# A stack of four graph layers on one core: the third layer's new rows are transposed by SyncE's transfers, and the two products behind them change places

## The reference

```python
h = relu(layernorm(x)); x = x + attention(h, adj)               # 4 heads
h = relu(layernorm(x)); x = x + (h @ W_self + (adj @ h / deg) @ W_neigh)
h = relu(layernorm(x)); x = x + gru(relu((adj @ h) @ W_msg.T + b_msg), h)
h = relu(layernorm(x)); x = x + hyperbolic(h, adj)
```

## Time and profile before

| | |
|---|---|
| median of three runs | 601.5 us (601.31 to 602.59) |
| the profiled execution | 602.1 us |
| its span | 600.3 us |
| TensorE busy | 560.5 us, 93% of the span |
| VectorE busy | 338.8 us, 56% |
| ScalarE busy | 211.4 us, 35% |
| GpSimd busy | 100.1 us, 17% |
| third layer with this pattern | about 310 to 450 us |

### The profile page before, as it was taken

One profiled execution on the slowest core, in us unless ns is written; L12 is line 12 of the kernel. 1 busy time (PEld: TensorE's weight loads), 2 busy tenths in 40 slices (PEclk: granted clock), 3 DMA queues, 4 the chain that ended last, 5 costly groups with the idle time before them and its releaser, 6 DMA issues.

```text
span 600.3 us, 12084 instructions
## 1 busy us (share of the span) xinstructions
PE 560.5 (93%) x4535; PEld 351.5 (59%) x4535; DVE 338.8 (56%) x1483; ACT 211.4 (35%) x580; POOL 100.1 (17%) x104
## 2 busy tenths in 40 slices
PE   4679899999999999999999999999999999999981
PEld 3578799999994544444444545554554444555540
DVE  4882372333323563333314687788779763676876
ACT  4530011100011110000032478778778555532433
POOL 3870100000000010000001112212122210330322
PEclk9979999999999999999999999999999999999996
DMA  8999999999940000000000001100100020110000
GB/s 230 108 108 108 106 109 108 108 108 108 109 44 4 5 14 0 1 0 1 19 0 19 18 26 30 36 13 25 36 1 20 17 86 3 36 55 36 18 36 35
DMA packets 23897, 29.17 MB, mean 49 GB/s; under 512 B 11296, under 2 KB 11936, under 8 KB 23840
## 3 DMA queue, kind: packets, MB, share of 16 engines
q0 software_dynamic: 8704, 16.78, 27.8%
q1 hardware_dynamic: 15136, 11.62, 6.4%
HBM read 72.43 MB, written 4.19 MB: 128 GB/s over the span
## 4 chain that ended last, share of the span: by engine, by line
PE 82%; DVE 10%; issue 3%; POOL 1%; ACT 1%; DMA 1%; SPq 0%; DVEq 0%; POOLq 0%
PE acc L1565 50%; PE acc L1375 9%; PE acc L1376 9%; PE acc L1405 4%; PE acc L1412 3%; PE acc L1395 1%; PE acc L1463 1%; PE acc L1462 1%; PE acc L1461 1%; DMA x<-x_rows 1%; POOL rs L1029 1%; PE acc L1497 1%; DVE hs_a L372 1%; PE acc L1468 1%; DVE mean L414 1%
## 5 line engine op out<-in xcount | busy, mean ns | idle before, releaser
L1565 PE MATMUL acc<-adj,hs_a 128*128 128x512 fp8e4 x1024 | 227.7, 379 | 2.8 <-DVE hs_a L561 2.0
L1565 PEld LDWEIGHTS acc<-adj,hs_a 128*128 128x128 f16 x1024 | 99.3, 98 | 116.7 <-DVE hs_a L561 2.2
L1375 PE MATMUL acc<-region_op,adj 128*128 128x133 f16 x1024 | 127.1, 224 | 5.0 <-issue 3.6
L1376 PE MATMUL acc<-region_op,adj 128*128 128x132 f16 x1024 | 127.2, 223 | 0.0
L1565 PE MATMUL acc<-adj,region_op 128*128 128x512 fp8e4 x512 | 118.3, 379 | 0.0
L1375 PEld LDWEIGHTS acc<-region_op,adj 128*128 128x128 fp8e4 x1024 | 100.9, 99 | 6.5 <-issue 3.7
L1376 PEld LDWEIGHTS acc<-region_op,adj 128*128 128x128 fp8e4 x1024 | 100.8, 98 | 0.1
L1565 PEld LDWEIGHTS acc<-adj,region_op 128*128 128x128 f16 x512 | 49.3, 98 | 56.7 <-issue 4.0
L1029 POOL TENSOR_TENSOR region_st<-region_st,small 128x4 f32<-128x4 f32 (+1 forms) x39 | 44.9, 1151 | 204.3 <-ACT w L1167 131.3
L1029 POOL TENSOR_TENSOR rs<-rs,small 128x4 f32 (+3 forms) x27 | 30.9, 1147 | 267.9 <-DVE rs L389 251.4
L1146 ACT ACTIVATE hs_a<-rowbuf 128x512 f32 (+1 forms) x8 | 5.0, 630 | 117.3 <-DVE rowbuf L395 117.3
(11 more groups left out here) (239 smaller groups left out, 682.7 us busy)
## 6 DMA issues: line engine op xcount, KB each, us to landing
adj<-adj_pieces POOLq DMA_DIRECT2D x32, 512.0 KB, 66.2
p_rows<-rowbuf SPq DMA_DIRECT2D x8, 256.0 KB, 2.0
region_op<-p_rows SPq DMA_DIRECT2D x8, 256.0 KB, 3.1
out_rows<-x SPq DMA_DIRECT2D x7, 256.0 KB, 2.0
x<-x_rows SPq DMA_DIRECT2D x3, 512.0 KB, 7.6
region_st<-matrices SPq DMA_DIRECT2D x1, 768.0 KB, 9.8
x<-x_rows SPq DMA_DIRECT2D x2, 256.0 KB, 4.4
hT<-region_op SPq DMA_TRANSPOSE x32, 2.3
```

Of the source, the lines that this page charges most:

```text
L1375: mm(bank[TG + it % TG][:, 0:HI], adj8[:, it, jt, :], op0[:, jt, 0:HI], start=(jt == 0), stop=False)
L1376: last = mm(bank[TG + it % TG][:, 0:LO], adj8[:, it, jt, :], op0[:, jt, HI:OPW], start=False, stop=(jt == NT - 1))
L1565: last = mm(dst, hs[:, jt, part, :], adj8[:, c * TG:(c + 1) * TG, jt, :], start=(k == 0), stop=(k == 2 * NT - 1))
```

## The change

For the groups 0 to 6 the eight transposes of the new rows are no longer matmuls and a copy but eight transposing transfers of SyncE from `row16` to `h3T16`, counted by a new semaphore `new_in`. They wait for `row16_ready` and for the embedding before (`emb_full`); in SyncE's stream they stand behind the store of the group before and ahead of the own rows of three groups later. Group 7 keeps TensorE's transposes and ScalarE's copy. Embedding and own product change places: `embed` at k = 50, `own_part` at k = 54, so behind `update_back` at 53. In the written out list both come behind 12 matmuls of the second aggregation of the last layer, and `update_back` of group 7 behind six of them. ScalarE's high half of a group's new rows waits until the transfers of the group before have landed.

```diff
+            def transpose_new_rows(g):
+                sp.wait_ge(S["row16_ready"], g + 1)
+                if g:
+                    sp.wait_ge(S["emb_full"], g)
+                for part in range(2):
+                    for t in range(TG):
+                        sp.dma_start(h3T16[:, part, t * D:(t + 1) * D], row16[:, part, t, :],
+                                     transpose=True).then_inc(S["new_in"], 16)
+
             sp.sem_inc(S["p1_out"], 16)
-            for g in range(NG):
-                transpose_own_rows(g)
-                if g > 2:
-                    store_p1(g - 3)
-            for g in range(NG - 3, NG):
-                store_p1(g)
+            transpose_own_rows(0)
+            transpose_own_rows(1)
+            for p in range(1, NG + 3):
+                if p >= 3:
+                    store_p1(p - 3)
+                if 0 <= p - 2 < NG - 1:
+                    transpose_new_rows(p - 2)
+                if p + 1 < NG:
+                    transpose_own_rows(p + 1)
...
             def high_rows(g):
                 act.wait_ge(S["xnew_ready"], g + 2 * NG + 1)
+                if g:
+                    act.wait_ge(S["new_in"], g * OWN_IN)
...
             def rows_T(g):
-                act.wait_ge(S["h3_tr"], g + 1)
+                act.wait_ge(S["h3_tr"], 1)
...
-                if second:
+                if i - 2 == NG - 1:
                     rows_T(i - 2)
...
+            def new_columns(s):
+                if s == 2 * NG - 1:
+                    pe.wait_ge(S["h3T_ready"], 1)
+                else:
+                    pe.wait_ge(S["new_in"], (s - NG + 1) * OWN_IN)
+
             def embed(s):
-                pe.wait_ge(S["h3T_ready"], s - NG + 1)
+                new_columns(s)
...
             def own_part(s):
-                pe.wait_ge(S["h3T_ready"], s - NG + 1)
+                new_columns(s)
...
-            late = {15: new_transposes, 43: own_part, 48: embed}
+            late = {50: embed, 54: own_part}
...
             aggregate(FIRST, 0, 36)
+            aggregate(SECOND, 0, 6)
+            update_back(FIRST - 1)
+            aggregate(SECOND, 6, 12)
+            embed(FIRST - 2)
             own_part(FIRST - 2)
-            embed(FIRST - 2)
-            update_back(FIRST - 1)
-            aggregate(SECOND, 0, 40)
+            aggregate(SECOND, 12, 40)
```

More of the change, by code:

```diff
@@ L233, in build_graph_stack @@
             "top_ready", "topall_ready", "w16_ready", "odd_ready", "odd_sum", "flag_ready", "turn", "gen_in",
-            "pre_tr", "pre_hT", "hidden_full", "sum_ready", "agg_full", "aThi_ready", "aT_ready", "l1_self", "self_read", "l1_neigh",
+            "pre_tr", "pre_hT", "hidden_full", "new_in", "sum_ready", "agg_full", "aThi_ready", "aT_ready", "l1_self", "self_read", "l1_neigh",
             "msg_full", "msg_ready", "gates_full", "rz_ready", "t_ready", "n_ready", "u_ready", "uT_full",
```

## The result

The changed kernel is **slower**: 604.3 us (median of 20 runs) beside 601.4 us for the kernel before (20 runs), ratio 1.0051 with a 95% interval of 1.0035 to 1.0068, so about 3.1 us. I had forecast 0.7 us less, 600.8, in a range up to 603.0. It went the way of rival C. The profiled executions have spans of 603.2 and 600.3 us.

What follows compares the result with a forecast made beforehand. TensorE was taken to bound the kernel, busy 93% of the span. Six periods each save 0.44 us less a 0.31 us wait, minus 0.05 for the order: 0.7 us less, 601.5 to 600.8, range 598.8 to 603.0.

Steps and rivals of the forecast that it cites:

- rival C: SyncE's queue, 97% occupied: closely packed sets take 10.68 us, each period 0.53 us longer; +3.2 us, 604.7; chance 0.17.
- The chain to the low half: VectorE's low half of the new rows, which releases the new transfers: no earlier step moves, ready at T0 + 4.94.
- T0: The first matmul of an aggregation on TensorE, from which the prediction counts the times in a period.
- An undisturbed set: SyncE's eight new transfers: start at T0 + 5.03, 10.02 us to issue, last landing T0 + 16.2; TensorE waits 0.31 us.
- Group 6's share: Handover to the next layer: TensorE waits for VectorE anyway, wait grows from 1.17 to 1.7 us, seventh 0.44 us lost.
- Its late embedding: Group 6's embedding, 3.8 us later: last rows start at T0 + 22.9 instead of 21.14, hidden before TensorE needs them.
- rival D: Handover slips: group 6's later embedding delays group 7's tangent, TensorE waits; price 0.3 to 1 us, about 601.5; chance 0.08.
- The queue's room: SyncE's queue: two sets and the store, 20.4 us plus 0.2 us waking, fit a period of 21.07 us.
- far bound: Upper limit for the new set's length on SyncE: the slowest set of the trace, 10.68 us, 0.66 us more.
- signs of being wrong: Low half at another distance from T0, a set other than 10.0 us, or VectorE taking TensorE's place in a period.
- The Trainium skill against the exchange: Page's 390 ns per transpose on TensorE against 1309 ns by DMA: speaks against the change; set estimated 0.4 us longer.

Runs made afterwards that it cites:

- the table of doses: Zero, 4, 6, 7 or 8 of a group's new-row transposes as transfers, against the kernel before: ratios 1.0003, 0.9971, 0.9966, 0.9972, 1.0051.

## Why the prediction was wrong

**What held.** TensorE bounds the stage and each transpose taken off it comes out at its full 0.44 us for eight (the table of doses). The chain to the low half is untouched (T0 + 4.96 for 4.94). An undisturbed set starts at T0 + 4.98 and is 10.03 us long, and the embedding behind it waits 0.22 us where I had 0.31. Group 6's share is lost at the handover, with a wait of 1.68 us for 1.7. Its late embedding passes 1.6 us on to the last rows (line 407 starts 6.74 us behind the last back transposes, 5.09 before), where I had 1.8, and ScalarE takes them up: its copy of group 7 starts 16.29 us behind them, 16.25 before. Behind the last back transposes both kernels take the same time, so rival D did not happen. The order and the handover cost 0.02 us in all.

**The step that failed is "The queue's room"**, in two terms. The first is a size. I had 20.4 us of issues and 0.2 us of waking. An undisturbed round, from the own set at 382.01 to the end of the new one, shows 10.10 + 0.58 + 10.03 and 0.26 us between them, and 20.97 us before it begins again: the store takes 0.58 us behind a transfer, not the 0.33 of the earlier trace rows where the queue had been idle. That leaves 0.1 us of the 21.07 and not 0.5, and of the period's own length nothing: period 4 took 20.98 us, and TensorE's own work is 20.76, less than SyncE's round. The second is a cause that I did not look for. The rows had one long set, 10.68 us, and I took it for a far bound, without a reason for it and with its weight put into a rival of 0.17. A look at the instruction queue at 297.6 would have pointed to the reason, and shown that one comes every 22 to 30 us; with the queue busy the whole time, four of them hit in six periods. Before, the five in the same stage all fell into pauses. This second term turned the sign: six periods like period 4, each 20.98 us for 21.20, would by estimate have made the stretch 1.3 us shorter.

The two together made the outcome. The long transfers add 0.86 + 0.50 + 0.94 + 1.13 = 3.4 us to SyncE's stream; the six waits beyond the undisturbed 0.1 to 0.3 us come to about the same, 3.7 us, because nothing of a lengthening is absorbed. (0.3 us more in period 2: the last transfer of that set, begun at 358.81, landed 2.7 us behind its issue, not 2.4. A packet of queue 14 stands beside it, at 359.78. Over the twelve traces, of the transfers with no packet of queue 8 from 0.9 us ahead of their start to 2.6 us behind it, 59 of the 93 with one of queue 14 between 0.5 and 2.1 us behind their start took over 2.55 us to land, and 7 of the 1005 others. No run moved these packets, so this is a coincidence seen often, not a cause shown.) Of the prediction's own signs of being wrong, a set other than 10.0 us long is the one that came.

**Rival C** had the right direction and half of the mechanism, longer sets in a queue without room: its price was 3.2 us, and the stretch shows 2.3, the ratio 3.1. It had the wrong cause. It made all sets equally slow because they lie close together, and the experiments exclude that: with own sets of four the long transfers are still there, and undisturbed sets in a full queue are 10.0 us. I also wrote that the sign turns 0.13 us beyond my count, and gave it a chance of 0.17 all the same; a forecast that rests on 0.1 us of slack in a resource filled to 97% by my own count should have had its slower case nearer to one in two.

**The Trainium skill against the exchange.** Its page VectorE: DVE Perf Modes, section The three transpose paths, with 1309 ns by DMA against 390 ns on TensorE, points to the right sign here, for another reason than its figures: undisturbed transfers took 1.25 us, and with seven of them the exchange pays.

**A slip that changed nothing.** The embedding's results came 3.9 us before the next T0 in the kernel before (16 matmuls and 0.44 us), not 3.7.

## What to carry to other kernels

Moving work from the bound engine to an idle queue pays by what it takes off the engine only while that queue keeps room; count the queue's issues as measured back to back, not after idle time, and leave it more than one disturbance of slack in each period (here about 1 us in 21). When the sum comes out at the edge, move most of the work and not all of it: seven eighths gave 2.3 us, eight eighths cost 2.3. And look up every outlier among the rows before it is used as a bound, in the queues beside it too: a rare long transfer is rare perhaps because the queue is rarely busy when its cause comes by.

## What the runs showed of the hardware

An instruction fetch of TensorE (16 KB for 256 instructions, about every 22 to 27 us here) that falls on a transposing transfer of SyncE's queue lengthens its issue from 1.23 to between 1.5 and 2.5 us, in 53 of 53 cases; which transfer it is depends on the number of TensorE's instructions before it, and moved by 11 to 15 us when 128 were added. A matmul of float32 is two matmuls and two weight loads in TensorE's stream (64 products, 256 instructions). A plain store of 256 KB takes 0.32 us to issue after idle time and 0.58 right behind a transposing transfer.
